# Two row halves and four row groups made pass by pass in the mixture stage of a five-stage kernel

## The reference, cut to what matters

```
logits = x @ gate_w.T + gate_b;  scores = softmax(logits)
top_v, top_i = top_k(scores, 2); val_sum = top_v.sum(-1)
for e in range(8):
    gate  = (top_i == e).sum(-1) * val_sum
    inter = x @ wi.T + bi + (x @ lora_A[e].T) @ lora_B[e].T      # 512 -> 2048
    out  += gate[..., None] * (relu(inter) @ wo.T + bo)          # 2048 -> 512
```

## Time and profile before

| what | value |
|---|---|
| median of three runs | 1252.92 us (1252.54 to 1254.14) |
| profiled execution, first to last instruction | 1248.6 us |
| profiled execution, its own time | not given apart from that span; 4.3 us lie between the span and the median |
| PE busy | 1202.0 us, 96% |
| DVE busy | 708.9 us, 57% |
| ACT busy | 520.2 us, 42% |
| mixture stage, hidden stretch | 1025.0 to 1144.5 us of the span |
| mixture stage, output stretch | 1144.5 to 1242.2 us of the span |

### The profile page before, as it was taken

How to read it: one execution, slowest core, us unless ns; L and a number is a source line. 1 busy time by engine, 2 the same in 40 slices (tenths; PEclk the granted TensorE clock), 3 DMA queues, 4 the chain that set the end, 5 groups by cost and what they waited for, 6 DMA issues and landing times.

```text
span 1248.6 us, 25643 instructions
## 1 busy us (share of the span) xinstructions
PE 1202.0 (96%) x10969; PEld 895.9 (72%) x10969; DVE 708.9 (57%) x1569; ACT 520.2 (42%) x1028; POOL 141.5 (11%) x164
## 2 busy tenths in 40 slices
PE   7999889999999999999999999999899999999997
PEld 5654478766466777777777777777787678888886
DVE  5456486767783555555555555555686755434432
ACT  3344447742132554545444444445453332222321
POOL 1300031166523000000000000000131100000000
PEclk9999999999999999999999999999999999999999
DMA  9669500201113110000010011110500201111210
GB/s 357 255 234 407 200 1 1 76 1 41 62 55 131 51 54 35 35 35 35 35 35 35 35 44 38 57 37 2 86 1 1 77 1 34 34 35 34 68 34 34
DMA packets 48485, 88.21 MB, mean 71 GB/s; under 512 B 19002, under 2 KB 20076, under 8 KB 44148
## 3 DMA queue, kind: packets, MB, share of 16 engines
q1 hardware_dynamic: 47024, 85.48, 19.4%
q10 hardware_dynamic: 1348, 1.09, 0.4%
HBM read 65.59 MB, written 20.97 MB: 69 GB/s over the span
## 4 chain that ended last, share of the span: by engine, by line
PE 88%; DVE 6%; ACT 3%; issue 1%; POOL 1%; DMA 1%; POOLq 0%; SPq 0%; DVEq 0%; ACTq 0%
PE bank L289 59%; PE bank L245 4%; PE bank L1790 3%; PE bank L1811 2%; PE bank L559 2%; PE bank L577 2%; PE bank L1138 2%; PE bank L1117 2%; PE bank L235 1%; DVE W L1380 1%; PE bank L495 1%; PE bank L2535 1%; PE bank L1086 1%; PE bank L1070 1%; PE bank L1094 1%
## 5 line engine op out<-in xcount | busy, mean ns | idle before, releaser
L2023 ACT ACTIVATE W<-W,low 128x512 f32<-128x512 f32 x128 | 90.9, 713 | 57.2 <-DVE low L1929 57.2
L2003 ACT ACTIVATE K<-bank,vecT 128x512 f32<-128x512 f32 x64 | 43.8, 689 | 167.0 <-PE bank L289 167.0
L225 POOL TENSOR_TENSOR rstd<-rstd,half_pow 128x1 f32<-128x1 f32 x48 | 30.9, 645 | 684.0 <-DVE rstd L221 684.0
L1902 DVE TENSOR_TENSOR W<-bank,vecT 128x256 f32<-128x256 f32 x16 | 6.8, 425 | 164.2 <-PE bank L1811 164.2
L1929 DVE CUSTOM_DVE_ANT_0 W<-bank,W 128x512 f32<-128x512 f32 x128 | 80.8, 687 | 30.6 <-PE bank L1790 30.6
L289 PE MATMUL bank<-xT,wT 128*128 128x512 f32 x384 | 92.8, 391 | 0.8 <-ACT W L2837 0.5
L289 PE MATMUL bank<-ctxT,Wkv 128*128 128x512 f32 x384 | 93.5, 396 | 0.0
L289 PE MATMUL bank<-Wq,Wkv 128*128 128x512 f32 x384 | 93.0, 394 | 0.0
L289 PE MATMUL bank<-Wkv,ctxT 128*128 128x512 f32 x384 | 92.9, 394 | 0.0
L289 PE MATMUL bank<-Wkv,Wq 128*128 128x512 f32 x384 | 92.1, 395 | 0.0
L289 PE MATMUL bank<-woT,hR 128*128 128x512 f32 x384 | 91.7, 394 | 0.1
(11 more groups left out here) (343 smaller groups left out, 2171.4 us busy)
## 6 DMA issues: line engine op xcount, KB each, us to landing
W<-ctx_turned SPq DMA_DIRECT2D x16, 1024.0 KB, 4.8
W<-in_ctx_dram SPq DMA_DIRECT2D x8, 1024.0 KB, 10.6
ctx_turned<-ctxT SPq DMA_DIRECT2D x8, 1024.0 KB, 7.6
ctx_turned<-W SPq DMA_DIRECT2D x8, 1024.0 KB, 6.6
XT<-in_ctx_dram SPq DMA_DIRECT2D x4, 1024.0 KB, 11.7
XT<-in_L_ffn_wi_dram SPq DMA_DIRECT2D x4, 1024.0 KB, 5.9
XT<-in_L_ffn_wo_dram SPq DMA_DIRECT2D x4, 1024.0 KB, 5.1
raw_own<-in_ctx_dram SPq DMA_DIRECT2D x3, 1024.0 KB, 10.7
```

Of the source, the lines that this page charges most:

```text
L225: pool.tensor_tensor(rstd[:, g:g + 1], rstd[:, g:g + 1], half_pow[:], ALU.pow).then_inc(rstd_ok.s, 1)
L2003: act.activation(K[:, m, :], bank[:, n % 4, :], ACT.Identity, bias=pcol("L1_xattn_bk", m)).then_inc(ring_a.s, 1)
L2023: act.activation(PR[:, j, :], PR[:, j, :], ACT.Exp, bias=low[:, j:j + 1], scale=-1.0, accum_out=total[:, j:j + 1]).then_inc(expd.s, 1)
```

## The change: what it does

A second helper, `products`, takes a list of banks and issues each pass for all of them before the next pass. It calls `before(i)`, a wait, just ahead of the first matmul into bank i.

hidden_pe, expert_pe and second_pe take a feature tile f and make both row halves, so the stationary tile of a pass serves two matmuls in a row, in two banks. The order on PE becomes: hidden_pe(0), router transposes, pick_chosen_pe(0), pick_chosen_pe(1), hidden_pe(1), expert_pe(0), then for f = 1 to 15 the turn of weight f + 1, hidden_pe(f) (for f from 2), second_pe(f - 1), expert_pe(f), and at the end second_pe(15). produce_pe makes its four row groups pass by pass, so they are finished by the last four matmuls. ACT and DVE take the weight splits one unit earlier, at odd u. All operations and their number stay.

```diff
+        def products(dsts, stationary, moving, steps, first=True, last=True, before=None):
+            passes = [(k, x, y) for k in range(steps) for x, y in ((0, 0), (0, 1), (1, 0))]
+            done = []
+            for n, (k, x, y) in enumerate(passes):
+                for i, dst in enumerate(dsts):
+                    if n == 0 and before is not None:
+                        before(i)
+                    ins = pe.matmul(dst, stationary(i, x, k), moving(i, y, k), start=(first and n == 0),
+                                    stop=(last and n == len(passes) - 1), skip_group_check=True)
+                    if n == len(passes) - 1:
+                        done.append(ins)
+            return done
...
-            def hidden_pe(f, n, u):
-                cols = slice(n * 512, (n + 1) * 512)
+            def hidden_pe(f):
                 pe.wait_ge(wt_v.s, wt_v(2 + f))
-                if u >= 4:
-                    pe.wait_ge(relu2.s, relu2(u - 4))
-                elif u >= 2:
-                    pe.wait_ge(pick_a.s, pick_a(u))
-                product(bank[:, hb(u), :], ..., C, last=False)
+
+                def room(n):
+                    u = N2 * f + n
+                    if u >= 4:
+                        pe.wait_ge(relu2.s, relu2(u - 4))
+                    elif u >= 2:
+                        pe.wait_ge(pick_a.s, pick_a(u))
+
+                products(both(f), ..., C, last=False, before=room)
...
+            def second_pe(f):
+                done = products(both(f), ..., 1, first=False,
+                                before=lambda n: pe.wait_ge(relu1.s, relu1(N2 * f + n)))
+                for ins in done:
+                    ins.then_inc(sec_pe.s, 1)
...
             def produce_pe(w):
-                for g in range(4):
+                def room(g):
                     if w == 0 and g == 2:
                         pe.wait_ge(joined.s, joined(N2 * FT - 1))
                     if f == 0 and n:
                         pe.wait_ge(xsum.s, xsum(5 * G + g))
-                    ins = product(bank[:, acc[g], :], ..., 1, first=(f == 0), last=(f == FT - 1))
+                done = products([bank[:, acc[g], :] for g in range(4)], ..., 1, first=(f == 0),
+                                last=(f == FT - 1), before=room)
...
-                hidden_pe(*tiles[0], 0)
+                hidden_pe(0)
...
                 pick_chosen_pe(0)
-                hidden_pe(*tiles[1], 1)
                 pick_chosen_pe(1)
-                for u in (2, 3):
-                    hidden_pe(*tiles[u], u)
-                for u in range(len(tiles) + 1):
-                    if u < len(tiles):
-                        if u >= 4:
-                            hidden_pe(*tiles[u], u)
-                        if u == len(tiles) - 1:
-                            turn_weight_pe(FT)
-                        expert_pe(*tiles[u], u)
-                    if u and u % N2 == 0 and u // N2 + 1 < FT:
-                        turn_weight_pe(u // N2 + 1)
-                    if u:
-                        second_pe(*tiles[u - 1], u - 1)
+                hidden_pe(1)
+                expert_pe(0)
+                for f in range(1, FT):
+                    if f + 1 < FT:
+                        turn_weight_pe(f + 1)
+                    if f >= 2:
+                        hidden_pe(f)
+                    if f == FT - 1:
+                        turn_weight_pe(FT)
+                    second_pe(f - 1)
+                    expert_pe(f)
+                second_pe(FT - 1)
...
-                    if u and u % N2 == 0 and u // N2 + 1 < FT:
-                        turn_weight_v(u // N2 + 1)
+                    if u % N2 == 1 and u // N2 + 2 < FT:
+                        turn_weight_v(u // N2 + 2)
```

More of the change, by code:

```diff
@@ L2536, in turn_weight_pe @@
                 ins.then_inc(wt_pe.s, 1)
-            def hidden_pe(f, n, u):
-                cols = slice(n * 512, (n + 1) * 512)
-                pe.wait_ge(wt_v.s, wt_v(2 + f))
-                if u >= 4:
-                    pe.wait_ge(relu2.s, relu2(u - 4))
-                elif u >= 2:
-                    pe.wait_ge(pick_a.s, pick_a(u))
-                product(bank[:, hb(u), :], lambda h, c: wT[:, f % 2, h, c * P:(c + 1) * P], lambda h, c: xT[:, h, c, cols], C,
-                        last=False)
@@ L2548, in expert_pe, with both @@
[L2548 to L2559, removed]
+            def both(f):
+                return [bank[:, hb(N2 * f + n), :] for n in range(N2)]
@@ new lines, in half_rows @@
+            def half_rows(n):
+                return slice(n * 512, (n + 1) * 512)
+            def hidden_pe(f):
+                pe.wait_ge(wt_v.s, wt_v(2 + f))
+                def room(n):
[4 more added lines that the diff above has]
+                        pe.wait_ge(pick_a.s, pick_a(u))
+                products(both(f), lambda n, h, c: wT[:, f % 2, h, c * P:(c + 1) * P],
+                         lambda n, h, c: xT[:, h, c, half_rows(n)], C, last=False, before=room)
@@ new lines, in expert_pe, with ready @@
+            def expert_pe(f):
+                def ready(n):
+                    if f == 0:
+                        pe.wait_ge(z_v.s, z_v(2 * n + 1))
+                done = products(both(f), lambda n, h, _: BT[:, h, f * P:(f + 1) * P],
+                                lambda n, h, _: z[:, 0, h, half_rows(n)], 1, first=False, before=ready)
+                for ins in done:
+                    ins.then_inc(hid_pe.s, 1)
+            def second_pe(f):
+                done = products(both(f), lambda n, h, _: BT[:, h, f * P:(f + 1) * P],
+                                lambda n, h, _: z[:, 1, h, half_rows(n)], 1, first=False,
+                                before=lambda n: pe.wait_ge(relu1.s, relu1(N2 * f + n)))
+                for ins in done:
+                    ins.then_inc(sec_pe.s, 1)
@@ L2569, in produce_pe @@
                         pe.wait_ge(xsum.s, xsum(5 * G + g))
-                    ins = product(bank[:, acc[g], :], lambda h, _: hR[:, w % 2, h, g * P:(g + 1) * P],
-                                  lambda h, _: woT[:, f, h, :], 1, first=(f == 0), last=(f == FT - 1))
-                    if f == FT - 1:
+                done = products([bank[:, acc[g], :] for g in range(4)], lambda g, h, _: hR[:, w % 2, h, g * P:(g + 1) * P],
+                                lambda g, h, _: woT[:, f, h, :], 1, first=(f == 0), last=(f == FT - 1), before=room)
+                if f == FT - 1:
+                    for ins in done:
                         ins.then_inc(prod.s, 1)
-                if f < FT - 1:
-                    ins.then_inc(prod.s, 1)
+                else:
+                    done[-1].then_inc(prod.s, 1)
             def pick_chosen_pe(n):
@@ L2852, in scalar @@
                         act.activation(h1[:, u % 2, :], bank[:, hb(u), :], ACT.Relu, bias=pcol("L1_ffn_bi", f)).then_inc(relu1.s, 1)
-                    if u and u % N2 == 0 and u // N2 + 1 < FT:
-                        turn_weight_a(u // N2 + 1)
+                    if u % N2 == 1 and u // N2 + 2 < FT:
+                        turn_weight_a(u // N2 + 2)
                 for w in range(1, N2 * FT):
```

1 line of the change is left out of this document (added).

## The result

The changed kernel takes 1273.8 us (median of four runs, 1273.5 to 1274.2) against 1252.7 for the kernel before (four runs, 1250.3 to 1254.1): ratio 1.0153, 95% interval 1.013 to 1.0177. It is 1.5% slower, a clear difference and in the direction forecast, but by 21 us and not by 14, and the time lies above the range (1259.5 to 1271). Two later comparisons of the same two kernels gave 1.0142 (1.0119 to 1.0165) and 1.0129 (1.0105 to 1.0153), that is 17 us.

A forecast was written before the change was run, and what follows sets the result against it. TensorE was taken as the bound, with matmul times unchanged; new waits of 6.1, 1.3, 3.7, 1.8 and 1.4 us, less 0.3, gave +14.0: span 1262.6, plus 4.3, 1266.9 us. Range 1259.5 to 1271.

The forecast's parts named there:

- Start: Start of the hidden stretch, hidden_pe(0) to second_pe(0): later pick copies and relu waits cost 1.3 us, bounds 0.5 to 2.5.
- Iterations: hidden_pe(2) to (15) wait for DVE's second relu: ten at 0.25 us, four with bias addition at 0.91, sum 6.1 us.
- End of the hidden stretch: second_pe(15) waits for ACT's relus, the first output product for the last join: 3.7 us, bounds 2.5 to 4.5.
- Between the halves: Output halves: four sums finish together and DVE frees banks one by one, delaying the next half's fifth matmul: 1.8 us.
- Last sums: End of the output: the four last sums end 2.54 us after the last matmul's start instead of 1.18: 1.36 us.
- the 0.3 that I took off: Hidden stretch: before was taken to hold some such waiting already, so 0.3 us was subtracted from the sum of 14.3.
- Rival 1: All 960 matmuls: new bank or stationary order makes them faster, 12.9 us at the column bound; 6%, beyond 209.5 ns 2%.
- the 216 ns: Skill's figure per 512-column matmul against 227 in the trace; reaching it would lower the sum some 10 us.
- the 4.3 us: Distance from profiled span to the median of 1252.9 us, added to the forecast span 1262.6 to give 1266.9.
- Rival 3: Clock falls once or twice in a seam, at pick copies or last relus, up to 1.7 us each: 1268.6 to 1270.3; 9%.
- Rival 4: Clock falls repeatedly, one short pause in each iteration: 14 x 1.7 = 24 us, 1291 us; 1%.
- Rival 2: Only the seams cost; DVE's relu and bias additions are in time in every iteration: 14.0 - 6.1 gives 1260.8; 10%.

The follow-up runs named there:

- experiment 5: Changed kernel with both DVE relus ahead of both joins; start, last feature tile, output steps 0 and 15 in the old order: ratio 1.0003, stage 260.5 us.
- Experiments 2: Kernel before with only the hidden part changed (PE order, pairs, weight splits), output as before: ratio 1.0094, stage 272.7 us.
- 3: Kernel before with only the output changed (the helper and produce_pe): ratio 1.0042, stage 265.5 us.
- 4: Changed kernel with DVE taking both relus of a feature tile before both joins: stage 270.9 us, iteration 8.65 us.
- 6: Changed kernel with the bias additions to X moved behind the second join: stage 274.07 us against 276.84 on the same terms.
- 7: Changed kernel with output steps 0 and 15 made group by group, the other 28 pass by pass: stage 272.4 us against 276.8.
- the control: Kernel before, run again with no edit: ten runs between 1248.4 and 1258.5 us, profiled span 1257.2, first part 994.5, stage 262.7.
- experiment 10: Changed kernel with unused matmuls added in the pauses at both ends of the hidden stretch: four runs 1263.1 to 1271.7 us, stage 277.3.

## Why the prediction was wrong

**Right: direction, places and nearly the size of the waits.** The stage became 15.3 us longer where 14.0 were forecast. Term by term, from the trace of after. *Start:* the turn of weight 3 begins 1034.43 - 994.31 = 40.1 us into the stage; before, the point with the same work less one second product (0.68) lies 1025.18 - 986.03 = 39.2 in: 1.65, forecast 1.3. *Iterations:* from the turn of weight 3 to that of weight 16 it takes 1158.67 - 1034.43 = 124.24 us; before, the same stretch takes 1144.46 - 1025.18 = 119.28 us with six matmuls (1.36) more: 6.3, forecast 6.1. Four iterations take 9.53 and nine 8.88 against 8.65; the last has no turn ahead of the pause, and its second matmul starts 0.58 us late. *End of the hidden stretch:* from its turn to the next but one 12.5 us, less 8.48: 4.0, forecast 3.7. *Between the halves:* the fifth matmul of the next half starts 2.86 us after the last of the first instead of 1.13: 1.7, forecast 1.8. *Last sums:* from the last matmul's start to the end 8.45 us instead of 6.87: 1.6, forecast 1.4. Sum 15.3. The waits measured are 1.0 more than the 14.3 of the forecast, and the 0.3 that I took off as waiting already in before was not waiting: experiment 5, where PE is never idle, has the same 8.65 us per iteration. One step has no row in the prediction: the second relu starts 0.61 us after the join, where it gives 0.66 to 0.68 for independent work. The trace of after has 1161.86 - 1161.25 = 0.61. Experiments 2 and 3 gave the two halves of the sum, 4 and 6 the iterations, 7 the output's seams.

**Right: the order of passes is free.** Experiments 5 and 7 show 0.227 us per matmul over two and over four banks. Rival 1 falls, and so does its bound of 12.9 us. Neither the 216 ns nor the 131 ns of the Trainium skill (TensorE: Matmul & The Clock Gate, Back-to-back issue gap) was met in any order tried here.

**Wrong: the base.** The step that failed is the last of the sum, where +14.0 is added to the profiled span "with the 4.3 us between the profiled span and the median". It puts the difference of the four unchanged stages at nothing. Of the 6.9 us by which 1273.8 lies above 1266.9, 1.3 come from the waits and 5.6 from this base. I took the 4.3 us for a fixed surplus of a run over its span. They are not: the profiled run of after took 1273.53 us with a span of 1272.2, so the surplus is 1.3. The other 3.0 us are probably falls of the clock that the three runs had and the profiled execution had not; the clocks of the three are not on record. The profiled execution of before was one with few falls, some 1250 us in its own time, 3 us below the three runs shown. And I let three runs that lay within 1.6 us stand for a kernel that spreads over 12. The execution of before that had the falls of after's first part is the control, with a span of 1257.2: 1257.2 + 14.0 + 1.3 = 1272.5 us is what the forecast gives for such an execution, and with the measured 15.3 it is 1273.8.

**Missing from the range: the clock in the stages that do not change.** I allowed the clock to fall in the new pauses and not where the earlier trace rows show it whole. The page of before has one fall at 877 and one at 986 us; the control of the same kernel has four in the first 300 us and twice the length near 880. With a base of 1248 to 1261 the same 14 us give 1262 to 1275, which the range should have held.

**Rival 3, the clock at the seams, came true,** though I gave it 9%: in all five traces of after the clock falls at hidden_pe(1) and at the end of the hidden stretch, and experiment 10 shows that they come from the pauses. The price was put too high: part of a fall lies in time in which PE waits anyway. Instead of 1.7 us each, filling the pauses won 0.3 us net at the end and 0.3 to 0.5 at the start, no more than profiles of one kernel differ. These two falls do not explain the miss.

**Rival 4 fell.** The clock is 1.00 in the whole stretch 1034.6 to 1158.8, over fourteen pauses. The oscillation that the Trainium skill describes (TensorE: Matmul & The Clock Gate, A second HAM failure mode: psum-queue depth-cycling) did not come here, from pauses that cost 0.2 to 0.9 us each. Rival 2 fell with the iterations of 8.88 and 9.53 us.

## What to carry to other kernels

A new order of matmuls on a bound TensorE is worth only what its spacing shows, and here no succession of banks or stationary tiles changed it; what the order does change is when results come, and results that arrive together make their readers queue. Count the work between a bank's last write and its next one in the new order, and look what else stands between the readers in their own queues: four bias additions of 0.66 us each, moved away, were worth 2.8 us.

Before a base is added to a sum, look at its clock and at more than three executions, and do not read the distance from one profile to a median as overhead.

## What the runs showed of the hardware that was not expected

The kernel before, unchanged on one core, takes 1248 to 1261 us, and its mean granted clock goes from 0.998 to 0.988 with it. The falls to half clock are 3.4 us long, or 6.8 where two follow one another, and come near 52, 144, 260, 267, 877, 882, 889 and 986 to 994 us of the span; which of them come differs between executions, and goes with where the others of the same trace lie. A fall of 3.4 us costs up to 1.7 us (8.5 us for 17 us more at half clock in the control), some 1.3 at the head of the stage, and less where PE waits. The Trainium skill (TensorE: Matmul & The Clock Gate, What's actually happening) says that the window in which the activity is watched is free-running, and that the count of cold matmuls at the start of one and the same kernel varies between runs. The eight traces of the two kernels agree in that the falls lie at other places from one execution to the next, with 986.0 to 994.5 us for the same first part; the cause that the page names is not shown by them.
